# Half a step of an attention pipeline, reordered: squares first, exponential, norms and scaling half a step later

## The reference, cut to what matters

```python
xn = cat(x[..., :64], shift_by_one_token(x[..., 64:]))
q, k, v = split(xn @ Wqkv)                      # 16 heads of 64
q = q / max(norm(q), 1e-12) * q_scale           # per token and head
k = k / max(norm(k), 1e-12) * k_scale
q = q * cos * scale + rotate_half(q) * sin * scale
k = k * cos / scale + rotate_half(k) * sin / scale
# windows of 32 queries, each with 64 keys (its own window and the one before)
sim = einsum('bhwie,bhwje->bhwij', q, k) * 8    # masked outside the band
out = einsum('bhwij,bhwje->bhwie', softmax(sim), v)
x = x + out @ Wo
```

## Time and profile before

| | |
|---|---|
| time, median of 3 runs | 3870.03 us (3869.78 to 3876.5) |
| the profiled execution's own time | 3872.81 us |
| its span | 3871.0 us |
| mean granted clock of TensorE | 0.971 |
| PE busy | 3542.8 us (92%) |
| PEld busy | 2679.4 us (69%) |
| ACT busy | 3021.4 us (78%) |
| DVE busy | 2948.5 us (76%) |
| POOL busy | 2494.8 us (64%) |

### The profile page before, as it was taken

One profiled execution on the slowest core, in us unless ns is written; L12 is line 12 of the kernel. 1 busy time (PEld: TensorE's weight loads), 2 busy tenths in 40 slices (PEclk: granted clock), 3 DMA queues, 4 the chain that ended last, 5 costly groups with the idle time before them and its releaser, 6 DMA issues.

```text
span 3871.0 us, 95171 instructions
## 1 busy us (share of the span) xinstructions
PE 3542.8 (92%) x30888; PEld 2679.4 (69%) x30894; DVE 2948.5 (76%) x4344; ACT 3021.4 (78%) x6096; POOL 2494.8 (64%) x2313
## 2 busy tenths in 40 slices
PE   5898679999889999889999899999799999799998
PEld 3444357777567777577777577776577777577776
DVE  4666378886788886788886788886788886788876
ACT  3556478887688887688887698886688886788885
POOL 3555377775377774577773577773677772677762
PEclk8999799999999999999999899999899999899999
DMA  4223200000100000000001000001000001000002
GB/s 134 86 91 94 55 2 1 0 0 1 30 2 0 0 0 22 9 2 0 0 0 30 2 2 0 0 0 30 2 1 0 0 1 29 2 1 0 0 1 72
DMA packets 59745, 67.76 MB, mean 18 GB/s; under 512 B 12006, under 2 KB 40164, under 8 KB 58468
## 3 DMA queue, kind: packets, MB, share of 16 engines
q1 hardware_dynamic: 59492, 64.64, 5.8%
HBM read 46.27 MB, written 18.35 MB: 17 GB/s over the span
## 4 chain that ended last, share of the span: by engine, by line
ACT 37%; issue 25%; PE 21%; DVE 12%; ACTq 2%; POOL 2%; DMA 1%; SPq 0%; DVEq 0%; POOLq 0%
PE bank L401 18%; ACT sb_area L790 18%; ACT bank L790 5%; DVE sb_area L1280 4%; ACT sb_area L940 4%; DVE sb_smax L1277 4%; ACT sb_lnb L952 3%; ACT sb_lnb L949 3%; ACT sb_area L983 2%; PE bank L673 1%; DVE sb_area L1155 1%; DVE sb_area L1257 1%; PE bank L614 1%; DVE sb_ssq L1267 1%; DMA sb_wqk_lo<-qk_rows 1%
## 5 line engine op out<-in xcount | busy, mean ns | idle before, releaser
L790 ACT ACTIVATE sb_area<-bank 128x512 f32<-128x512 f32 (+4 forms) x2149 | 1335.2, 648 | 209.4 <-PE bank L401 154.9
L1257 DVE TENSOR_TENSOR sb_area<-bank,sb_rots 128x1024 f32<-128x1024 f32 x768 | 939.1, 1225 | 393.7 <-ACT sb_area L940 392.9
L1520 POOL TENSOR_TENSOR sb_area<-sb_area,sb_rn 128x512 f32<-128x512 f32 x768 | 785.7, 1044 | 586.3 <-ACT sb_rn L956 586.3
L401 PE MATMUL bank<-sb_area 128*64 128x64 f32 (+6 forms) x17104 | 1062.2, 275 | 21.2 <-ACT bank L790 8.7
L1506 POOL TENSOR_TENSOR sb_area<-sb_area 128x512 f32<-128x512 f32 x768 | 969.4, 1280 | 86.6 <-DVE sb_area L1257 84.8
L401 PEld LDWEIGHTS bank<-sb_area 128*64 128x64 f32 (+4 forms) x17104 | 746.9, 145 | 283.1 <-issue 229.5
L401 PE MATMUL bank<-sb_wqk_hi,sb_xwin 128*128 128x512 f32 x1536 | 723.6, 473 | 55.7 <-DVE sb_xwin L1237 47.6
L401 PE MATMUL bank<-sb_area,sb_wvo 128*128 128x256 f32 x3072 | 728.3, 381 | 3.1 <-DVE sb_xT L1312 3.1
L401 PEld LDWEIGHTS bank<-sb_area,sb_wvo 128*128 128x128 f32 x3072 | 555.0, 190 | 78.4 <-issue 12.8
L614 PE MATMUL bank<-sb_ident,sb_area 128*128 128x128 f32 x3072 | 488.4, 282 | 39.9 <-ACT sb_area L790 31.2
L614 PEld LDWEIGHTS bank<-sb_ident,sb_area 128*128 128x128 f32 x3072 | 354.6, 143 | 235.6 <-issue 124.8
(11 more groups left out here) (115 smaller groups left out, 3979.4 us busy)
## 6 DMA issues: line engine op xcount, KB each, us to landing
qk_rows<-sb_p SPq DMA_DIRECT2D x52, 256.0 KB, 4.2
sb_wqk_hi<-qk_rows SPq DMA_DIRECT2D x32, 256.0 KB, 2.9
sb_wqk_lo<-qk_rows SPq DMA_DIRECT2D x32, 256.0 KB, 2.7
sb_area<-in_Wqkv SPq DMA_DIRECT2D x7, 1024.0 KB, 6.1
sb_area<-in_WvT SPq DMA_DIRECT2D x7, 512.0 KB, 7.4
sb_wo_bd<-in_Wo SPq DMA_DIRECT2D x14, 256.0 KB, 8.3
sb_area<-in_x SPq DMA_DIRECT2D x4, 512.0 KB, 6.1
sb_area<-in_x SPq DMA_DIRECT2D x8, 256.0 KB, 2.9
```

The lines of the kernel that those rows point to most:

```text
L401: return nc.tensor.matmul(o, a, b, start=start, stop=stop, skip_group_check=True)
L790: return nc.scalar.activation(o, i, ACT.Copy)
L1257: tt_(t12[:, c % 2, :, :].rearrange("p u (h d) -> p u h d", h=8), src, bc(rots[:, tt, s, :, :], [P, 2, 8, D], 2), ALU.mult).then_inc(S["ro ...
L1520: pt_(qn[:, c, :].rearrange("p (h d) -> p h d", h=8), qsum[:, c % 2, :].rearrange("p (h d) -> p h d", h=8), r, ALU.mult).then_inc(S["qn"], 1)
```

## The change

In a half step ACT now does both squares first, then `exp` and `norms` of the half before (their lags go from 2 and 0 to 3 - wp and 1 - wp, of the other half), then `turned_qk(2*wp)`, then `mask_ahead`, also with the lag of the half before, and then the rest. PE does `project(2*wp+1)` ahead of `turn_p`, and `windows` moves to the second half. DVE does the two rotations ahead of `sums`. POOL does one `add` ahead of the scalings and writes the sums straight into `qn`, where `scale` then works in place; `qn` has six chunks and `sqb` four, `qsum` is gone. The rotation table has no place of its own any more: it is loaded with each layer's weights, in two transfers, into the part of `kT` that is free then.

```diff
-        sqb, t12 = take(2, 512), take(2, 2, 512)
-        qsum, qn = take(2, 512), take(4, 512)
+        sqb, t12 = take(4, 512), take(2, 2, 512)
+        qn = take(6, 512)
...
         kT = take(HP, WIN + T)
+        rot = [kT[:, 4 + s, WIN:WIN + T].rearrange("p (t u d) -> p t u d", t=TT, u=2) for s in range(2)]
...
+        def qk_place(c, tt):
+            return c // 2 if c % 2 == 0 else 2 + c - 1 + tt % 2
...
-            sp.dma_start(rot[:, :, :, :], ins["c_rot"]).then_inc(S["const"], 16)
...
+                for s in range(2):
+                    sp.dma_start(rot[s], ins["c_rot"][:, :, s, :, :]).then_inc(S["w_loaded"], 16)
...
-                        if c == 1:
+                        if c == 3:
                             pe.wait_ge(S["xwev"], g_of(bt) * 4 + tt + 1)
...
-                        pe.wait_ge(S["ev"], g * 4 + 1)
+                        pe.wait_ge(S["ev"], g * 4 + 3)
...
                         project(2 * wp)
                         turn_qk(2 * wp)
+                        project(2 * wp + 1)
                         turn_p(wp)
-                        project(2 * wp + 1)
                         score(wp)
-                        if wp == 0:
+                        if wp == 1:
                             windows()
...
-                        act.wait_ge(S["ssq_raw"], g)
-                        nc.scalar.activation(sqb[:, c % 2, :], pj[c % 2][:, :], ACT.Square).then_inc(S["sq"], 1)
+                        act.wait_ge(S["ssq_raw"], g + 1 - c % 2)
+                        nc.scalar.activation(sqb[:, c, :], pj[c % 2][:, :], ACT.Square).then_inc(S["sq"], 1)
...
                     for wp in range(2):
                         square(2 * wp)
+                        square(2 * wp + 1)
+                        exp(3 - wp, 1 - wp)
+                        norms(1 - wp, 1 - wp)
                         turned_qk(2 * wp)
+                        mask_ahead(3 - wp, 1 - wp)
                         turned_p(wp)
-                        square(2 * wp + 1)
-                        if wp == 0:
+                        if wp == 1:
                             windows()
-                            if not (part == 0 and t == 0) and (v := behind(t, i, part, -1)):
-                                heads_of_tokens(*v)
+                        elif not (part == 0 and t == 0) and (v := behind(t, i, part, -1)):
+                            heads_of_tokens(*v)
                         weighed(4 - wp, 1 - wp)
                         turned_qk(2 * wp + 1)
-                        exp(wp)
-                        mask_ahead(wp)
-                        norms(wp)
...
-                        sums(3 - wp, 1 - wp)
                         rotate(2 * wp)
                         rotate(2 * wp + 1)
+                        sums(3 - wp, 1 - wp)
...
-                        pool.wait_ge(S["qn"], g + 5)
+                        if c % 2 == 0:
+                            pool.wait_ge(S["tr"], g)
...
                     for wp in range(2):
-
+                        add(2 * wp)
                         scale(1 - wp, 2 - 2 * wp)
                         scale(1 - wp, 3 - 2 * wp)
                         normalise(3 - wp, 1 - wp)
-                        add(2 * wp)
                         add(2 * wp + 1)
```

More of the change, by code:

```diff
@@ L36 @@
 MASKED = -1.0e30
-AREA = 25856
+AREA = 26880
 OUT_PARTS = (((6, 3), (5, 1)), ((5, 2), (4, 0)))
@@ L156, in build @@
         kT = take(HP, WIN + T)
+        rot = [kT[:, 4 + s, WIN:WIN + T].rearrange("p (t u d) -> p t u d", t=TT, u=2) for s in range(2)]
+        first_kept = at[0] - 4 * (WIN + T)
         assert at[0] <= AREA
@@ L182, in build @@
         xres = take(2, TT, C)
-        assert at[0] <= AREA
+        assert at[0] <= first_kept
         xb = ysum
@@ L407, in split3 @@
                 return mm(o, a_lo, b_hi, False, True)
-            pe.wait_ge(S["const"], 9 * 16)
+            pe.wait_ge(S["const"], 8 * 16)
             for b in range(B):
@@ L613, in turn_qk @@
                         for j in range(4):
-                            m = nc.tensor.transpose(rbank[:, j * P:(j + 1) * P], qn[:, c, j * P:(j + 1) * P],
+                            m = nc.tensor.transpose(rbank[:, j * P:(j + 1) * P], qn[:, qk_place(c, tt), j * P:(j + 1) * P],
                                                     ident[:, :])
@@ L901, in heads_of_weights @@
             def heads_of_weights(l):
[L902 removed]
+                act.wait_ge(S["w_loaded"], (l + 1) * (7 * 16))
                 for c in range(4):
@@ L938, in square, with norms @@
                         act.wait_ge(S["proj"], g + 1)
-                        act.wait_ge(S["ssq_raw"], g)
-                        nc.scalar.activation(sqb[:, c % 2, :], pj[c % 2][:, :], ACT.Square).then_inc(S["sq"], 1)
-                    def norms(half):
-                        if not (v := behind(t, i, part, 0)):
+                        act.wait_ge(S["ssq_raw"], g + 1 - c % 2)
+                        nc.scalar.activation(sqb[:, c, :], pj[c % 2][:, :], ACT.Square).then_inc(S["sq"], 1)
+                    def norms(lag, half):
+                        if not (v := behind(t, i, part, lag)):
                             return
@@ L976, in turned_qk, with exp @@
                         m.then_inc(S["ev"], 1)
-                    def exp(wp):
-                        if not (v := behind(t, i, part, 2)):
+                    def exp(lag, wp):
+                        if not (v := behind(t, i, part, lag)):
                             return
@@ L983, in exp, with mask_ahead @@
                         nc.scalar.activation(dd[:, wp, :], dd[:, wp, :], ACT.Exp).then_inc(S["exp"], 1)
-                    def mask_ahead(wp):
-                        if not (v := behind(t, i, part, 2)):
+                    def mask_ahead(lag, wp):
+                        if not (v := behind(t, i, part, lag)):
                             return
@@ L1109, in _ @@
             column = iter(range(28))
-            for name, n in (("sq", 1), ("rotd", 1), ("ssq_raw", 1), ("add", 1), ("tr", 3), ("score", 2), ("yy", 2),
+            for name, n in (("sq", 1), ("rotd", 1), ("ssq_raw", 3), ("add", 1), ("tr", 3), ("score", 2), ("yy", 2),
                             ("pt", 2), ("qn", 6), ("ln_part", 3), ("pn", 1), ("oo", 1)):
@@ L1197, in prepare_weights @@
             def prepare_weights(l):
-                dve.wait_ge(S["w_loaded"], (l + 1) * (5 * 16))
+                dve.wait_ge(S["w_loaded"], (l + 1) * (7 * 16))
                 for c in range(4):
@@ L1266, in square_sums @@
                         dve.wait_ge(S["ln_part"], g_of(bt) * 8 + 2 * tt + half)
-                        nc.vector.tensor_reduce(ssq[:, tt % 2, half, :], sqb.rearrange("p c (h d) -> p (c h) d", h=8), AX.X, ALU.add)\
+                        nc.vector.tensor_reduce(ssq[:, tt % 2, half, :], sqb[:, 2 * half:2 * half + 2, :].rearrange("p c (h d) -> p (c h) d", h=8), AX.X, ALU.add)\
                             .then_inc(S["ssq_raw"], 2)
```

18 lines of the change are left out of this document (8 added, 10 removed).

## The result

The changed kernel takes 5519.24 us (median of four runs, 5460.51 to 5530.0), the kernel before 3870.49 (3869.78 to 3876.5). The ratio is 1.421, its 95% interval 1.4112 to 1.4307. The forecast was 5530 us in a range of 4900 to 6120. The profiled execution of the changed kernel is the fastest of its runs: 5460.51 us, span 5458.1, mean granted clock 0.839.

A forecast was written before the change was run, and what follows sets the result against it. PE, busy 196.0 of 200 us, was taken as nearest its limit, ACT (179.2) next. 3872.8 plus 1047 for the chain plus 612 for the clock made 5532 us for the profiled execution, 5530 for the median; range 4900 to 6120.

The forecast's parts named there:

- The mechanism: Each half, score on PE waits 2.85 or 3.42 us for ACT's mask, queued behind squares, exp, norms and turned_qk.
- The size of the chain: Projection, ACT's pieces and scores in series: a step of 20.44 us against 14.2, 1047 us in six layers.
- The size of the clock term: After each half's pause PE runs 3.4 us at clock 0.50, costing 1.7 us; 612 us in all.
- What was put at zero: Among others the rotation table's transfers, -14 to +8 us, and emptying the pipeline, 0 to 30 us, each taken as 0.
- emptying the pipeline: Moved exp and mask lengthen a layer's last six steps by 0 to 5 us, 30 in all; taken as 0.
- The transfers and places: Rotation table loaded with each layer's weights, between -14 and +8 us, taken as 0; sqb of four chunks adds no instruction.
- The first: Rival: PE's stalls for the mask come but the clock holds at full; 4917 us, chance 0.15.
- The second: Rival: PE's clock stays low for two stretches after each stall; 6110 us, chance 0.18.
- The third: Rival: ACT runs ahead, the mask is not late, PE loses its 0.27 us wait a step; 3820 us, chance 0.02.
- The fourth: Rival: PE has a fifth in hand and catches up; 4434 us at full clock, 5046 with the 612; chance 0.14.

The follow-up runs named there:

- e1_mask_first: Changed kernel with ACT doing exp and the mask first in a half, ahead of both squares; 3928.21 us, ratio 1.0148.
- e5_before_mask_late: Kernel before with only mask_ahead moved from the end of a half to behind the second square of the next half; 4622.59 us, ratio 1.1947.
- e3_pe_filled: Changed kernel with ten plain matmuls added on PE ahead of the transposes of turn_p; 4924.1 us, ratio 1.2726.
- e8_turned_before_norms: e1_mask_first with turned_qk(2*wp) ahead of norms on ACT; 3841.97 us, ratio 0.9919.
- e4_places_only: Changed kernel's places, transfers and sums in place, with the order of the kernel before on PE, ACT, DVE and POOL; 3875.26 us, ratio 1.0009.
- e10_pool_order: e8_turned_before_norms with POOL's order of before, both scalings and normalise ahead of the first add; 3831.22 us, ratio 0.9899.

## Why the prediction was right

**The mechanism** held in each part named ahead: the scores' idle time (1044 us; a pause was 2.53 us in one half, less than the 2.8 to 3.4 named), its releaser, ACT idle ahead of its second square, a step above 20 us, a clock well below 1.00. `e1_mask_first` takes the late mask away and nearly all of the loss with it; `e5_before_mask_late` brings in that alone and gets the loss.

**The size of the chain** was taken a little long. 20.44 us a step were forecast; the pieces of the timelines above, at full clock, are these. From the second half's scores to the next projection 1811.96 to 1817.74, 5.78 (forecast 6.02); to its square 0.98 (1.02); projection to square in the other half 1.02 (1.02); square to scores 1809.04 to 1811.96, 2.92 (3.15). The next first half's scores start at 1822.33, 3.61 after the square (3.72). With the forecast's 5.51 for the stretch that ran at half clock this makes 19.82. `e3_pe_filled` has, over its full steps, 19.8 as well. ACT's instructions follow each other more closely than my sum had them: `turned_qk` 0.48 where I took 0.57, mask to scores 0.64 where I took 0.73. A stall is thus 2.85 on the mean, not 3.14. Thirty steps lost 160.5 us, not 174.5: in six layers 84 us less than forecast.

**The size of the clock term**: forecast 3.4 us a step, 102 a layer. A full step lost 23.38 less 19.82, 3.56 us, and the layer shown 99.9. Right in sum, but not as told: I took one stretch of 3.4 us behind each pause, while in the traces some pauses have a longer one behind them (3.70 us at 0.50 and then 5.60 at 0.83) and some none. The clock of 200 us is 0.82, not 0.85.

**What was put at zero**: step 1 to step 2 of a layer, while the pipeline fills, takes 16.7 us in that layer after (1335.38 to 1352.11) and 11.4 before (1626.27 to 1637.68): 5.3 us a layer, 32 us in six layers. Not all of it is the stall: `windows` stands half a step later now, and in `e8_turned_before_norms`, which has no stall, the same interval is 13.0 (1619.17 to 1632.14). The prediction gave 0 to 30 us to emptying the pipeline and had no term for filling it. The transfers and places were nothing, as `e4_places_only` shows.

The forecast for the profiled execution, 5532, was 71 us too high: 84 too much for the chain and about 13 for the clock, against 32 left out, which is 65. Three of the six layers took 682.6 to 682.7 us and not the 686.5 shown, 11 us more, so the sum closes to about 5 us. That the median came within 11 us of the forecast is partly luck: the profiled execution is 59 us below the median of its runs, whose spread (1.3%) is wider than that of the kernel before (0.2%). What makes them differ was not tried; the longer ones show a mean granted clock of 0.824 to 0.826, the profiled one 0.839.

**The rivals.** The first (chain, but the clock holds, 4917 us) is what `e3_pe_filled` made on purpose, 4924.1; without the added matmuls it does not come. The second (two stretches at half clock each time) is refuted by the steps above. The third (the mask is early, the wait ahead of the windows goes, 3820 us) is wrong for the change, yet it is what the change would have been with ACT's list in another order: `e8_turned_before_norms` and `e10_pool_order`, 3842 and 3831. The fourth, PE with a fifth in hand, falls twice: at full clock the stretch from scores to projection took 5.78 us, not the 4.8 that four fifths of 6.02 would be, and in `e8_turned_before_norms` PE is busy for 199.10 of 200 us with weight loads at 158.75 and a full step does not get below 14.1 us, nor in `e10_pool_order`. For this kernel the matmuls' busy time is the better measure of how near the limit PE is. The Trainium skill (Trainium Kernel Development and Optimization, Performance Expectations), as the prediction weighed it, holds the weight loads' share for the better one; here the measurement decides.

## What to carry to other kernels

When work is moved by half a step, ask of each instruction which result of the same half it now stands behind, on its own engine's list, and who needs it in that half: a producer that passes from "written half a step ahead" to "written behind the projection of this half" turns two busy engines into one chain. Sum that chain from starts in the trace, and add what such pauses do to PE's clock, here 100 of 260 us a layer. If the late work is wanted, put the instructions on which the bottleneck waits ahead of those that only POOL waits for; the same pieces then gave 0.7 to 1.0% instead of costing 42%.

## What the runs showed that I had not expected

**PE's clock fell behind some pauses and not behind others, and matmuls of no use held it up.** That it would fall was forecast, not this. Pauses of 1.35 and 1.26 us twice a step left it at 1.00; pauses of 2.5 to 3.2 us brought it to 0.82 on the mean; of two pauses of 1.89 us in `e5_before_mask_late` one left it and one did not, so the length of a pause alone does not tell; plain matmuls inside the same pause, with 1.02 and 0.30 us of it left, brought it back to 1.00 and were worth 595 us.

**DVE's small instructions stretch beside POOL's.** In the earlier trace rows DVE was busy for 170.88 of 200 us, in `e1_mask_first` for 190.36 with as many instructions to a step. In the kernel before the copies fall into a pause of POOL (its `add` ended at 1313.87, its next instruction came at 1315.07), on DVE's timeline:

```profile
1313.98 0.21 DVE L1229 COPY sb_xs<-sb_xT 64x128 f32 x1
1314.20 0.22 DVE L1230 COPY sb_xs<-sb_xT 64x127 f32 x1
```

In `e1_mask_first` the same copies and the subtraction behind them, on DVE's timeline:

```profile
1406.06 0.21 DVE L1234 COPY sb_xs<-sb_xT 64x128 f32 x1
1406.28 1.22 DVE L1235 COPY sb_xs<-sb_xT 64x128 f32 x1
...
1413.15 1.36 DVE L1242 TENSOR_TENSOR sb_xwin<-sb_xs,sb_xwin 128x128 fp32r<-128x128 f32 x1
```

and POOL's timeline beside them:

```profile
1406.09 1.33 POOL L1512 TENSOR_TENSOR sb_area<-sb_area 128x512 f32<-128x512 f32 x1
...
1413.07 1.29 POOL L1512 TENSOR_TENSOR sb_area<-sb_area 128x512 f32<-128x512 f32 x1
```

The second copy ends at 1407.50, POOL's `add` at 1407.42; the subtraction ends at 1414.51, the other `add` at 1414.36. Here a DVE instruction that comes just behind the start of POOL's lasts until POOL's is over, 1.2 to 1.4 us instead of 0.2 to 0.3. The Trainium skill (SBUF — State Buffer, Who interferes with whom) says that the two share a pair of ports under an exclusive lock: for a copy in certain modes whoever issues first has it for the whole instruction, and a DVE instruction with two inputs in SBUF contends with one of POOL's that reads SBUF. These rows agree with it. The cause is read from times that match; no run took POOL's work away. It costs this kernel nothing that a run showed, since DVE is not what PE waits for.
